# A graph network on one core: q, k and v from split f32r weights, a GpSimd split, and a reordered first stage

## The reference, cut to what matters

```python
q = (x @ Wq + bq).reshape(N, H, HEAD)       # N = 512, H = 8, HEAD = 64; x = relu(layernorm(x))
k = (x @ Wk + bk).reshape(N, H, HEAD)
v = (x @ Wv + bv).reshape(N, H, HEAD)
scores = jnp.einsum('nhd,mhd->nhm', q, k) / np.sqrt(HEAD)
adj = jnp.zeros((N, N)).at[edge_index[0], edge_index[1]].set(1.0)
scores = jnp.where(adj[:, None, :] == 0, -1e9, scores)
attn = jax.nn.softmax(scores, axis=1)
attn_out = jnp.einsum('nhm,mhd->nhd', attn, v).reshape(N, D_OUT) @ Wo + bo
```

## Time and profile before

| | us |
|---|---|
| three runs, median (lowest to highest) | 495.31 (494.41 to 497.62) |
| the profiled execution, its own time | 495.8 |
| its span in the profile | 494.0 |
| busy in it: TensorE matmuls, VectorE, ScalarE, GpSimd | 450.1, 345.2, 230.4, 19.1 |

### The profile page before, as it was taken

How to read it: one execution, slowest core, us unless ns; L and a number is a source line. 1 busy time by engine, 2 the same in 40 slices (tenths; PEclk the granted TensorE clock), 3 DMA queues, 4 the chain that set the end, 5 groups by cost and what they waited for, 6 DMA issues and landing times.

```text
span 494.0 us, 6104 instructions
## 1 busy us (share of the span) xinstructions
PE 450.1 (91%) x2182; PEld 271.0 (55%) x2182; DVE 345.2 (70%) x753; ACT 230.4 (47%) x405; POOL 19.1 (4%) x43
## 2 busy tenths in 40 slices
PE   1699999989778799999999899799989899999997
PEld 1343433443223243784447577578647478888885
DVE  4687887799999778914687785558687858585312
ACT  4697884676696642323113234444563352511210
POOL 3110000001000000010000000000000000000000
PEclk9999999999999899999999999899999899999999
DMA  8982444205999974975029949460597404000002
GB/s 284 344 348 90 167 130 157 99 1 196 389 419 417 389 287 167 391 302 193 0 74 392 386 170 361 171 250 27 229 409 252 172 21 172 1 0 1 1 1 85
DMA packets 18456, 98.14 MB, mean 199 GB/s; under 512 B 3711, under 2 KB 4095, under 8 KB 7935
## 3 DMA queue, kind: packets, MB, share of 16 engines
q1 hardware_dynamic: 14871, 73.58, 39.3%
q0 software_dynamic: 3552, 24.12, 12.8%
HBM read 92.45 MB, written 5.24 MB: 198 GB/s over the span
## 4 chain that ended last, share of the span: by engine, by line
PE 67%; DMA 15%; DVE 10%; ACT 4%; issue 2%; SPq 1%; DVEq 0%
DMA bring<-in_basis 13%; PE bank L1191 12%; PE sbank L1508 9%; PE bank L1260 7%; PE sbank L1243 6%; PE bank L1521 6%; PE sbank L1177 6%; PE bank L1408 6%; PE bank L1493 4%; PE bank L1227 3%; DMA alph<-in_alphas 3%; PE bank L1177 2%; PE sbank L1367 2%; DVE stat L717 2%; PE sbank L1161 2%
## 5 line engine op out<-in xcount | busy, mean ns | idle before, releaser
L712 DVE TENSOR_SCALAR cnt<-iota_row,edge_f 128x512 bf16<-128x512 f16 x132 | 41.0, 346 | 4.5 <-PE sbank L1243 4.5
L1177 PE MATMUL sbank<-bring,attw 120*32 120x512 f32 x320 | 40.6, 617 | 2.7 <-DMA bring<-in_basis 2.7
L377 ACT ACTIVATE stat<-stat 128x1 f32<-128x1 f32 x32 | 6.5, 202 | 57.6 <-DVE stat L720 57.5
L407 ACT ACTIVATE s<-bank,colsb 128x512 f32<-128x512 f32 x24 | 16.5, 687 | 35.8 <-PE bank L1191 35.8
L1243 PE MATMUL sbank<-cnt,adjT 128*128 128x512 bf16 x132 | 30.3, 381 | 1.7 <-DVE cnt L712 1.7
L1177 PE MATMUL bank<-bring,attw 120*32 120x512 f32 x192 | 24.2, 618 | 8.3 <-DMA bring<-in_basis 8.2
L1260 PE MATMUL bank<-hT,wring 128*128 128x512 f32 x64 | 30.6, 623 | 0.0
L464 ACT ACTIVATE adjT<-distance,edge_w,edge_f 128x128 bf16<-128x128 bf16 x61 | 29.2, 479 | 1.4 <-PE sbank L1243 1.4
L1110 DVE SCALAR_TENSOR_TENSOR y_lo<-sbank,gate,y_hi 128x512 fp32r<-128x512 f32 x16 | 11.8, 749 | 22.6 <-ACT y_hi L639 22.5
L439 ACT ACTIVATE distance<-iota_row,edge_f 128x128 bf16<-128x128 f16 x61 | 24.4, 401 | 4.5 <-DVE edge_f L756 2.8
L709 DVE TENSOR_SCALAR adjT<-iota_row,edge_f,edge_w 128x128 bf16<-128x128 f16 x71 | 21.8, 307 | 6.4 <-PE sbank L1243 6.4
(11 more groups left out here) (209 smaller groups left out, 1014.6 us busy)
## 6 DMA issues: line engine op xcount, KB each, us to landing
bring<-in_basis SPq DMA_DIRECT2D x63, 1024.0 KB, 8.3
wring<-in_weights POOLq DMA_DIRECT2D x8, 1024.0 KB, 9.3
w_scratch<-stage SPq DMA_DIRECT2D x64, 64.0 KB, 6.3
hT<-in_weights POOLq DMA_DIRECT2D x4, 1024.0 KB, 5.1
landing<-in_weights POOLq DMA_DIRECT2D x4, 1024.0 KB, 8.6
qkw<-w_scratch POOLq DMA_DIRECT2D x2, 2048.0 KB, 8.7
rring<-in_rows POOLq DMA_DIRECT2D x12, 256.0 KB, 7.6
xr<-in_x SPq DMA_DIRECT2D x4, 256.0 KB, 4.3
```

The lines of the kernel that those rows point to most:

```text
L712: dve.tensor_scalar(hot_s[:, n % HOT, :], iota[:, :], src_f[:, n:n + 1], None, ALU.is_equal).then_inc(sem("hot_ready"), 1)
L1177: mm = pe.matmul(unit_bank(b)[32 * j:32 * j + 32, :], attw[0:KB, u // UNITS, g, :], bring[0:KB, u % BATCH, j, :], start=(g == 0), stop=(g ...
```

## The change

The tiles of q, k and v are computed from f32r parts of h and of the weights: 12 f32r matmuls a tile. h's high part is ScalarE's copy of the transposed block, its low part a new VectorE subtraction (`h0T_lo`). q's high parts are four copies by GpSimd, its low parts four subtractions by VectorE ahead of the loop; all parts of k and v are made by GpSimd (four copies and four subtractions each), k's after its row loads, v's after the last q tile. The low parts overwrite the weights (v's high part goes over q's low one), h's parts lie in `landing` and `hT`. The three edge loads are issued by ScalarE in the place of SP. ScalarE turns block c - 1 right after it has made h's block c, ahead of the first distance. `never` and `bq8` move from before the loop to its chunk 8. The loads of f1a and f1b are swapped. VectorE waits for the k tiles before it writes the digits, which share memory with k's parts.

```diff
--- before.py
+++ after.py
@@ -97,7 +97,7 @@
              "c2_1": ("weight_parts", 5 * C), "gcn": ("weight_parts", 6 * C),
              "root1": ("c2_1_psum", C), "root2": ("c2_1_psum", C)}
 
-T_ORDER = ("h1T", "hT2", "agg0", "agg1", "agg2")
+T_ORDER = ("hT0", "h1T", "hT2", "agg0", "agg1", "agg2")
 
 
 ROWS = ("bv", "bo", "g1", "be1", "b2", "g2", "be2", "lin_b", "lin_a", "gcn_b", "bias1", "bias2")
@@ -137,7 +137,7 @@
 
         xr = sb("xr", [P, C, D])
         hr = sb("hr", [P, C, D])
-        hT = sb("hT", [P, C, D])
+        hT, hT_r = places([("hT", [P, C, D], F32)], [("hT_r", [P, C, D], F32R)])
 
 
         qkw, hT_hi, hT_lo = places(
@@ -184,6 +184,8 @@
             [("root_hi", [P, C, D], F32R), ("root_lo", [P, C, D], F32R)])
 
         x_hi, x_lo = root_hi, root_lo
+        h0_hi, h0_lo = y1_lo, hT_r
+        qkv_parts = {"q": (y0_hi, w0_hi), "k": (y0_lo, w0_lo), "v": (w0_hi, w1_hi)}
         Y_parts = ((y0_hi, y0_lo), (y1_hi, y1_lo))
         src_f, dst_lo, rel1, field, minus_w = (edge_f[:, a, :] for a in range(5))
         weight_f = edge_w[:, :].bitcast(F32)
@@ -270,8 +272,6 @@
 
                 for c in range(C):
                     sp.dma_start(xr[:, c, :], x[:, c, :]).then_inc(sem(f"x{c}_loaded"), 16)
-                for i, e in enumerate((src, dst, etype)):
-                    sp.dma_start(edge_i[:, i, :], e).then_inc(sem("edges_loaded"), 16)
                 sp.dma_start(colsb[:, :], cols).then_inc(sem("cols_loaded"), 16)
                 sp.dma_start(alph[:, :], alphas.partition_broadcast(P)).then_inc(sem("cols_loaded"), 16)
                 sp.wait_ge(sem("att_ready"), 1)
@@ -321,6 +321,19 @@
 
                 for i in range(4):
                     pool.dma_start(weight(WEIGHTS[i]), weights[i]).then_inc(sem(f"weight_{i}_loaded"), 16)
+                def high_part(name, k):
+                    pool.tensor_copy(qkv_parts[name][0][:, k, :], weight(name)[:, k, :]).then_inc(
+                        sem("qkv_hi"), 1)
+
+                def low_part(name, k):
+                    hi, lo = qkv_parts[name]
+                    pool.wait_ge(sem("qkv_hi"), "qkv".index(name) * C + k + 1)
+                    pool.tensor_tensor(lo[:, k, :], weight(name)[:, k, :], hi[:, k, :].bitcast(F32),
+                                       ALU.subtract).then_inc(sem("qkv_parts"), 1)
+
+                need_weight(pool, "q")
+                for k in range(C):
+                    high_part("q", k)
                 pool.wait_ge(sem("att_loaded"), 16 * 2 * Q)
                 for g in range(1, BATCH):
                     pool.tensor_copy(attw[0:KB, :, g, blk(Q, g)], attw[0:KB, :, 0, 0:Q]).then_inc(
@@ -329,6 +342,18 @@
                     pool.dma_start(row(ROWS[i]), rows[i, :].partition_broadcast(P)).then_inc(
                         sem(f"row_slot{i}_loaded"), 16)
 
+                for name in "kv":
+                    need_weight(pool, name)
+                    if name == "k":
+                        pool.wait_ge(sem("qkv_parts"), C)
+                    else:
+                        pool.wait_ge(sem("q_psum"), C)
+                    high_part(name, 0)
+                    for k in range(1, C):
+                        high_part(name, k)
+                        low_part(name, k - 1)
+                    low_part(name, C - 1)
+
                 def load_weight(name):
                     i = WEIGHTS.index(name)
                     last, tiles = LAST_READ[name]
@@ -351,8 +376,8 @@
                         pool.wait_ge(sem("gcn_psum"), C)
                     pool.dma_start(qkw[:, :, :], scratch[layer]).then_inc(sem("w_loaded"), 16)
 
+                load_weight("f1b")
                 load_weight("f1a")
-                load_weight("f1b")
                 load_row("g2", "v")
                 load_weight("f2a")
                 load_row("be2", "h_plus_bo")
@@ -441,6 +466,8 @@
 
 
                 my_chunks = [n for n in range(ECH) if on_act(n)]
+                for i, e in enumerate((src, dst, etype)):
+                    act.dma_start(edge_i[:, i, :], e).then_inc(sem("edges_loaded"), 16)
                 root(0, 0)
                 for c in range(C):
                     if c + 1 < C:
@@ -448,11 +475,12 @@
                     act.wait_ge(sem("nbias0"), c + 1)
                     act.activation(hr[:, c, :], xr[:, c, :], ACT.Relu, scale=st(0, c, 9),
                                    bias=st(0, c, 10)).then_inc(sem("h0"), 1)
+                    if c:
+                        turn("hT0", h0_hi, c - 1)
+                turn("hT0", h0_hi, C - 1)
                 act.wait_ge(sem("edge_step"), 8)
                 act.wait_ge(sem("iota"), 1)
                 distances(0)
-                for c in range(C):
-                    turn("hT0", hT, c)
                 for n in range(ECH):
                     if on_act(n):
                         i = act_hots(n)
@@ -731,12 +759,19 @@
                     dve.wait_ge(sem("v_psum"), c + 1)
                     dve.tensor_tensor(vr[:, c, :], bank[2 + c % 2][:, :], row("bv"), ALU.add).then_inc(sem("v"), 1)
 
+                def h0T_lo(c):
+                    dve.wait_ge(sem("T_hi"), c + 1)
+                    dve.tensor_tensor(h0_lo[:, :, blk(P, c)],
+                                      bank[4 + c % 2][:, :].rearrange("p (f n) -> p f n", f=C),
+                                      h0_hi[:, :, blk(P, c)].bitcast(F32), ALU.subtract).then_inc(sem("hT0"), 1)
+
                 for c in range(C):
                     dve.wait_ge(sem(f"x{c}_loaded"), 16)
                     norm_stats(0, xr[:, c, :], c)
                     if c:
                         nbias(0, c - 1)
                 nbias(0, C - 1)
+                h0T_lo(0)
 
                 dve.wait_ge(sem("edges_loaded"), 48)
                 dve.tensor_copy(src_f, edge_i[:, 0, :]).then_inc(sem("edge_step"), 1)
@@ -745,6 +780,7 @@
                 dve.tensor_scalar(dst_part[:, 1, :], edge_i[:, 1, :], P.bit_length() - 1, None,
                                   ALU.logical_shift_right).then_inc(sem("edge_step"), 1)
                 dve.tensor_scalar(rel1, edge_i[:, 2, :], 0.0, None, ALU.not_equal).then_inc(sem("edge_step"), 1)
+                h0T_lo(1)
                 dve.wait_ge(sem("edge_step"), 4)
                 dve.tensor_copy(dst_lo, dst_part[:, 0, :]).then_inc(sem("edge_step"), 1)
                 dve.scalar_tensor_tensor(field, rel1, float(C), dst_part[:, 1, :], ALU.mult, ALU.add).then_inc(
@@ -755,10 +791,12 @@
                 dve.wait_ge(sem("edge_step"), 7)
                 dve.tensor_scalar(minus_w[:, :], weight_f, -1.0, None, ALU.mult).then_inc(sem("edge_step"), 1)
                 dve.wait_ge(sem("iota"), 1)
-                dve.wait_ge(sem("ident"), 2)
-                dve.tensor_scalar(never[:, :], ident[:, :], NEVER, None, ALU.mult).then_inc(sem("never"), 1)
-                dve.wait_ge(sem("cols_loaded"), 32)
-                dve.tensor_scalar(bq8[:, :], col("bq", 0, C), HD ** -0.5, None, ALU.mult).then_inc(sem("bq8"), 1)
+                h0T_lo(2)
+                h0T_lo(3)
+                for k in range(C):
+                    dve.wait_ge(sem("qkv_hi"), k + 1)
+                    dve.tensor_tensor(w0_hi[:, k, :], weight("q")[:, k, :], y0_hi[:, k, :].bitcast(F32),
+                                      ALU.subtract).then_inc(sem("qkv_parts"), 1)
 
                 def plus_bo(c):
                     if c == 0:
@@ -768,6 +806,12 @@
 
                 for n in range(ECH):
                     one_hots(n)
+                    if n == HOT // 2:
+                        dve.wait_ge(sem("ident"), 2)
+                        dve.tensor_scalar(never[:, :], ident[:, :], NEVER, None, ALU.mult).then_inc(sem("never"), 1)
+                        dve.wait_ge(sem("cols_loaded"), 32)
+                        dve.tensor_scalar(bq8[:, :], col("bq", 0, C), HD ** -0.5, None, ALU.mult).then_inc(
+                            sem("bq8"), 1)
                     t, at = divmod(n - FIRST_TILE - TILE_LAG, TILE_EVERY)
                     if at == 5 and C <= t < 2 * C:
                         plus_bo(t - C)
@@ -775,6 +819,8 @@
                 dve.tensor_scalar(packed, bank[7][:, :], 2.0 ** UNIT_BITS, None, ALU.mult).then_inc(
                     sem("packed"), 1)
                 dve.wait_ge(sem("packed"), 1)
+
+                dve.wait_ge(sem("k_psum"), C)
 
                 def digit(f):
 
@@ -1246,18 +1292,20 @@
                 def qkv_tile(t):
 
                     which, c = divmod(t, C)
-                    w = weight("qkv"[which])
-                    if c == 0:
-                        need_weight(pe, "qkv"[which])
+                    w = qkv_parts["qkv"[which]]
                     if which == 1:
                         pe.wait_ge(sem("q"), c + 1)
                     elif which:
                         pe.wait_ge(*((sem("v"), c - 1) if c >= 2 else (sem("k"), C)))
                     at = 2 + c % 2 if which == 2 else c
                     for k in range(C):
```

(10 more changed lines are left out.)

## The result

The changed kernel took 499.84 us (median of 20 runs, 496.45 to 504.07) against 496.83 for the kernel before on the same chip: a ratio of 1.0056 with a 95% interval of 1.0032 to 1.0080, slower by 2.8 us by the ratio and by 3.0 by the medians. Every ratio here leaves out the runs in the chip's slower state (one of the changed kernel's 20 and eight of e6's twelve, for instance), so it can differ a little from that of the medians. I had forecast 488.8 and a range up to 499.0, so both the sign and the range were missed. The ratio applied to the 495.3 that the forecast started from gives 498.1, so 9.3 of the 11.0 us of the miss are the forecast's; the other 1.7 come almost wholly from the base, since the median of before's twenty runs is 1.5 above that of the three that the forecast started from.

What follows compares the result with a forecast made beforehand. TensorE was taken to set the pace, with VectorE having 10.9 us of slack. Tiles 6.3 plus start 0.6 made 6.9 us, giving 488.9 from 495.8 or 488.4 from 495.3; forecast 488.8, range 486.5 to 499.

Steps and rivals of the forecast that it cites:

- B: Loop: VectorE time taken by GpSimd's sixteen instructions; expected a few us, from 0 to 13.2, or 22 with dearer instructions.
- Rival 1: Loop: VectorE is blocked while GpSimd works; 7.9 us paid, net 1.0 us slower, 496.8; chance 0.27.
- The slack of 5.3: Loop: VectorE's idle time left as cover with the shorter tiles, 5.3 us, down from 10.9.
- Tiles: q, k and v tiles: 12 matmuls take 2.73 us, 0.70 less per tile; seven in the loop give 4.9.
- I keep the excess: First tile: stays 1.78 us longer than the others, as TensorE idles before it again; gain counted as 0.7.
- the sum of 6.3: Gain from tiles in us: 4.9 for seven in the loop, 0.7 for the first, 0.7 for one v tile.
- The start: Before the loop: one-hots begin at 17.0 against 17.64, 0.6 us gained; bounds 16.2 to 18.2.
- rival 3: Start: q parts end at 19 to 20, 1.4 to 2.4 us lost; chance 0.12 together with another rival.
- GpSimd's own durations: Loop: 0.55 us a copy and 1.1 a subtraction, 6.6 us for each group of eight.
- it moves forward as a whole: After the loop: everything is released by loop events, so all comes earlier, 6 to 7 us from the first score on.

Runs made afterwards that it cites:

- e6: The changed kernel with only k's split on GpSimd, v's eight instructions left out and v tiles reading q's parts; ratio 0.9937 to the kernel before.
- e1: The changed kernel without GpSimd's sixteen instructions for k and v, whose tiles read q's parts instead; 493.31 us, ratio 0.9869 to the kernel before.
- e3: The changed kernel with GpSimd's sixteen instructions spaced, each behind a further counting matmul; 493.21 us, ratio 0.9917 to the kernel before.
- e10: The changed kernel run once more, unedited, for a second profile; ratio 1.0061 to the kernel before.
- e2: The changed kernel with VectorE making k's and v's parts itself, one step after each of sixteen chunks; 495.21 us, ratio 0.9931 to the kernel before.
- e7: The changed kernel with GpSimd's sixteen instructions each waiting until VectorE has filled its ring; ratio 1.0064 to the kernel before.
- e11: e3 with f1a loaded ahead of f1b again; ratio 0.9959 to the kernel before.

## Why the prediction was wrong

**The step that failed** is "I take a B of a few us, under the slack, as the small copies are the only row with both engines at work". B was about 12 us (VectorE busy for 65.2 and 65.4 against 53.1 in before and 53.3 in e1), near the upper one of the bounds by 0.55 and 1.1 us and far from a few. That it lies so near 13.2 is in part luck: GpSimd's instructions lasted 15.0 and not 13.2, and VectorE lost four fifths of that and not all. The three 120x16 copies took 398 ns each and cost nothing that shows, and each moved a thirtieth of the data. That it is the data that keeps VectorE out, and not the time an instruction takes, fits both rows but was not tried at sizes between. The nearest row was near in engine and place but not in size, and I let it set the middle of the range.

The Trainium skill, "SBUF — State Buffer", section "Who interferes with whom", says that VectorE and GpSimd share one pair of ports, held by one of them alone. e3's pairs of rows agree (0.61 and 1.25 us for a 0.30 us one-hot), and so does the start: of VectorE's instructions that ran beside q's copies, three edge steps with operands in SBUF went from 0.22 to 0.64 us, while a subtraction with one operand in PSUM kept its 0.68. I had cited the rule and given it 0.27, with a row of another size as the reason against it.

**Rival 1** was the right mechanism and the nearest number: 496.8, a ratio of 1.002 to the profiled execution's 495.8, against 1.0056. It lacked 1.8 us. The slack of 5.3 was right: e1 has 4.9 us of idle time, and in e10, where none is left, a B of 12 less 5.3 makes 6.7, and its loop lost 6.3 to the forecast's sum. Two things of after are not in it. The slack doesn't cover a standstill: 3.0 us of VectorE's idle time were still there, as a one-hot of 6.66 us empties the rings whatever slack there is later. And TensorE, having waited 4.61 us, did its next tile in 4.73 and not 2.74, which no term held; in 30 to 40 us its granted clock was 0.66:

```profile
30.00:40.00 10.00, 8.12 (x27) 4.76 (x29) 9.20 (x32) 2.50 (x7) 1.51 (x2) 0.66 0.17 66
```

**Tiles**: 2.74 and 2.95 against 2.73 forecast and 0.70 for the v tile, right. The first tile gained nothing in after where I had 0.7: nearly all its matmuls stepped at 0.43, about half pace, and it took 5.23 against 5.21. In before only the first four of eight instructions were slow (0.85 from start to start for 0.43). So "I keep the excess" didn't hold there: the slow part lasted some 5 us and not 3.5. In e1 it was shorter, and the tile took 4.60, near the forecast. That is why e1's stretch met the sum of 6.3 within 0.1: 4.8 for the seven tiles, 0.7 for the v tile and 0.6 for the first, and 0.3 more since the first tile began sooner behind the first one-hot (0.72 us against 1.03).

**The start**: 18.38 against 17.0; rival 3's direction: 0.7 lost, where that had 1.4 to 2.4. x's first block landed at 4.83 against 3.92 before, three times the 0.3 that I had allowed, and GpSimd's copies of q took 3 x 0.41 from the edge steps:

```profile
4.83 0.69 DVE L745 BATCH_NORM_STATS2 stat<-xr 128x6 f32<-128x512 f32 x1 [4.83 <-DMA xr<-in_x]
...
10.99 2.37 POOL L325 CAST y_hi<-wring 128x512 fp32r<-128x512 f32 x4 [5.77 <-DMA wring<-in_weights]
...
11.13 0.64 DVE L778 TENSOR_SCALAR dst_part<-edge_i 128x132 int32<-128x132 int32 x1
...
11.69 0.63 DVE L780 TENSOR_SCALAR dst_part<-edge_i 128x132 int32<-128x132 int32 x1
```

The waits for the last edge load and for alphas went, as forecast, and starts from 17.4 to 18.9 over the kernels with this order show that its scatter is larger than the 0.6 that I had forecast as its gain.

**GpSimd's own durations**: 0.61 a copy and 1.26 to 1.30 a subtraction against 0.55 and 1.1. My estimate of 1.12 from the Trainium skill, "GPSIMD Engine Reference", section 3.1, was low by the same 0.15 or so.

**After the loop**: "it moves forward as a whole" held from the first projection on (316.7 and 316.8 us), not for the attention stage, which got 3.7 longer. That a stage behind the change would keep its length was assumed, with no row.

Put together: without the sixteen instructions the kernel gains 6.5 us by its ratio (e1), near the 6.9 of the forecast, and with them it loses 2.8. That they cost 9.3 us is shown, since e1 and after differ in them (and in the waits for them) alone. Where the 9.3 lie is shown for 6.4 to 9.2, in the loop; of the attention stage, 3 us longer in two profiles than in before's one and e1's one, the timed runs don't show the length. e1 also gave back 1.4 us in the score stage. Why the changed kernel meets the low clock in the attention stage more often than before is open, and e2 met it too. The mean clock of the timed runs was 0.986 to 0.988 for before, 0.978 for after, 0.977 for e10, 0.973 for e7 and 0.988 for e3; but it doesn't rank them, with 0.985 for e1, the fastest, and 0.983 for e2.

**The better versions.** Spaced (e3, 0.9917) and split by VectorE (e2, 0.9931), both with all of the computation, beat both kernels: by 0.7 to 0.8% the one before and, ratio over ratio, by 1.2 to 1.4% the changed one. Their intervals leave out 1, but e3's twin e11 came to 0.9959.

## What to carry to other kernels

Price wide work that is put on GpSimd at nearly its full length on VectorE's side (here 12 of 15 us back to back, 10 of 16 spaced) wherever VectorE reads and writes SBUF beside it, and take a row of the same size before trusting a cheap one. If the slack is in small pieces, space the work so that no single loss outlasts what the ring between the engines holds, and expect executions of the same kernel to differ where it isn't spaced; or let VectorE do it, if it is faster there. And a saving in one stage is safe only as far as the next stage's own bound, a DMA ring and the clock behind its waits, stays as it was.

## What was unexpected of the hardware

- Beside eight 128x512 GpSimd instructions with no gap between them one one-hot stood for 6.66 us in one execution of the changed kernel; in another the longest took 3.17, and beside the next eight none took over 1.44. So a VectorE instruction can stand through seven GpSimd instructions, and yet a gap isn't what it needs to get in.
- Beside a spaced 512-wide GpSimd instruction of 0.65 or 1.40 us a one-hot of 0.30 lost 0.3 or 0.95 us and ended 0.05 behind it; beside three copies of 120x16, 398 ns each, one-hots lost nothing that shows.
- Waits of TensorE of 1.9 to 2.6 us for a DMA were followed by basis and score matmuls at twice their duration in after (1.93 for 1.1, 2.01 for 1.06), with the granted clock at 0.66 and 0.70 over those 10 us, but not in e3 behind one of 1.94. Five matmuls of zeros ahead of such waits held it at 1.00, at the price of 2.4 us of TensorE's time a step; no gain in the total was seen.
- The first tile behind an idle TensorE ran at half pace (0.43 us from matmul to matmul and not 0.23) while the row of the granted clock for 20 to 30 us reads 1.00.
